# A four-direction scan whose directions run in an order that alternates with the image, with its input reloaded in blocks of 1024

## The chip, the core and the metric

The kernel runs on one core of one Trainium2 chip. The metric is the device time of one execution in microseconds (us); lower is better.

## What is computed

The input x is (8, 64, 64, 96): eight images of 64 x 64 pixels with 96 channels. Two layers are added to it, a selective scan block and a small resampling network. The change touches the scan alone, which in the reference is

```python
x_flat = xa.reshape(B, D_INNER, L)                       # B = 8, D_INNER = 192, L = 4096
x_wh = xa.transpose(0, 1, 3, 2).reshape(B, D_INNER, L)   # the same pixels by columns
x_hwwh = jnp.stack([x_flat, x_wh], axis=1)
xs = jnp.concatenate([x_hwwh, jnp.flip(x_hwwh, -1)], axis=1)   # four directions, K = 4
x_dbl = jnp.einsum('bkdl,kcd->bkcl', xs, x_proj_w)
delta = jax.nn.softplus(dts + dt_proj_b[None, :, :, None])
# each direction k, channel d, state n, along l:
h = dA * h + (dl * ul)[..., None] * Bl[:, :, None, :]
y = jnp.einsum('bkdn,bkn->bkd', h, Cl)
y = (y1 + y2 + y3 + y4)    # the four directions, turned back to row order
```

with 192 channels, 16 states, and `xs * Dk` added to each direction's y. Direction 0 goes along the rows forward, 1 along the columns forward, 2 along the rows backward, 3 along the columns backward.

## The kernel before

The program has three phases, one after the other. The first normalises x, makes `xa` (a convolution) and a gate, and leaves both in DRAM. The second, `scan_phase`, is the scan. The third adds the directions' results, projects, and computes the second layer.

**Steps and units.** The scan phase works through 256 steps in the order of the list `steps`: image b (8), direction k (4), chunk ci (4 chunks of 1024 positions), half (2 halves of 96 channels). A step is 12 units, one for each group g of 4 states and each third j of the 96 channels, 128 partitions x 1024 positions each. One image is 32 steps, one direction 8. The four directions of an image are called first to fourth here by their place in time; before the change they are k = 0, 1, 2, 3.

**A unit.** TensorE (PE) fills a PSUM tile with B spread over partitions (`fill`, the line with `selb`, L614, or with `diag`, L655 in six units of a pair of steps). VectorE (DVE) multiplies it by `dur` (L739), then scans it (L761). ScalarE (ACT) makes the decays `E` from `dlr` (L845). GpSimd (POOL) multiplies the scanned states by C (L945) and, in four units of a pair of steps, makes the product with `dur` itself into `dbu` (L937). PE sums the products of a group into `yps` (L677, in `sum_y`). Each engine works through a fixed order.

**sum_y.** For the first group of a step it begins with what is to be added to the scan's result: in direction k = 0 the skip term, a product of `dg` and `u` (L668, one call for each 512 columns); in directions k = 2 and 3, for which `second(m)` is true, the result of direction k - 2, which was stored in DRAM (`yk`) and is loaded back as `yp` (L671, also one call for each 512 columns). It stands ahead of the `fill` of a later unit on PE: at unit 5 of a step the order is fill(6), first half of `sum_y`, then fill(7), second half.

**u.** The tile `u` holds the whole of one image's `xa`, 96 partitions x 2 halves x 4096, and is not doubled. `project` (L599) reads it for B, C and dt of a chunk, POOL's `delta` (L928) for `dlu` = delta x u, and the skip term reads it. `load_u(b)` loads it with two DMAs of 1536 KB once all readers of the image before are through (`x_done`, `dlu_made`), and counts them on one semaphore, `u_in`.

**The DMA queue.** All DMAs of the scan are issued by SyncE (SP) in program order, and SP stands still where one has to wait: `out_dl` and `out_dlu` write delta and dlu of a step to DRAM, `in_dlr` and `in_dur` read them back spread over 128 partitions (4 DMAs of 384 KB each), `store_y` and `load_y` carry the results, each for the step that the loop of `sync` names. `load_u` of the next image stands in the next to last step of an image, between `out_dlu` and `in_dur` of the last step.

Of the kernel before, what the change touches and what calls it, by code (L numbers as in the profile page):

```python
# [13 lines left out]
NB = 8  # L14
HW = 64
L = HW * HW
C = 96
ND = 192
NS = 16
NK = 4  # L20
# [3 lines left out]
TC = 1024  # L24
# [284 lines left out]
def scan_phase(nc, ctx, T, S):  # L309
# [47 lines left out]

    steps = [(b, k, ci, half) for b in range(NB) for k in range(NK) for ci in range(NCH) for half in range(2)]
    NSTEP = len(steps)
# [5 lines left out]
    ve_set = sem("ve_set")  # L365
    u_in = sem("u_in")
    x_done = sem("x_done")
# [87 lines left out]
    def second(m):  # L455
        return steps[m][1] >= 2

# [3 lines left out]

    def ends_image(m):
        return m % (NK * 2 * NCH) == NK * 2 * NCH - 1

# [26 lines left out]
    def sync(e):  # L491
        for t, n in consts:
            e.dma_start(t, S[n]).then_inc(consts_in, 16)

        def load_u(b):
            if b:
                e.wait_ge(x_done, 16 * b)
                e.wait_ge(dlu_made, 32 * b)
            for h in range(2):
                e.dma_start(u[:, h, :], S["xa"][b, h]).then_inc(u_in, 16)  # L500

# [36 lines left out]
        def load_y(m):  # L538
            if m == NSTEP or not second(m):
                return  # L540
            b, k, ci, half = steps[m]
            t0 = t_of(k, ci)
            e.wait_ge(y_stored, 16 * (steps.index((b, k - 2, NCH - 1 - ci, half)) + 1))
            if seconds(m):
                e.wait_ge(yp_added, seconds(m))
            e.dma_start(yp[:], S["yk"][b, k % 2, half, :, t0:t0 + TC]).then_inc(yp_in, 16)

        load_u(0)
        for m in range(2):
# [4 lines left out]
        for n in range(NSTEP):  # L554
            if n % 2 == 0:
                if n:
                    in_dlr(n + 1)
                if n:
                    out_dlu(n + 1)
                if ends_image(n + 1) and n + 2 < NSTEP:  # L560
                    load_u(n // 32 + 1)
                if n:
                    in_dur(n + 1)
                if n:
                    store_y(n - 1)
                load_y(n + 1)
            else:
                if n + 1 < NSTEP:
# [15 lines left out]
    def tensor(e):  # L584
        def project(c, sub):
            b, k, ci, _ = steps[2 * c]
            t0 = t_of(k, ci) + sub * 512
            if sub == 0:
                if ("x", c) in held:
                    e.wait_ge(*held["x", c])  # L590
                e.wait_ge(u_in, 32 * (b + 1))
            o = stage[0:C + NR, sub * 512:(sub + 1) * 512]
# [66 lines left out]
        def sum_y(i, sub):  # L659
            m, g = divmod(i, NG)  # L660
            b, k, ci, half = steps[m]
            cols = slice(sub * 512, (sub + 1) * 512)
            if sub == 0 and g == 0 and m:
                e.wait_ge(y_copied, m)
            if g == 0 and k == 0:
                t0 = t_of(k, ci) + sub * 512
                e.wait_ge(skip_made, 3)
                e.matmul(yps[0:C, cols], dg[:, half, :], u[:, half, t0:t0 + 512], start=True, stop=False)  # L668
            if g == 0 and second(m):
                e.wait_ge(yp_in, 16 * (seconds(m) + 1))  # L670
                r = e.matmul(yps[0:C, cols], idn[0:C, 0:C], yp[:, cols], start=True, stop=False)  # L671
                if sub:
                    r.then_inc(yp_added)
            if sub == 0:
                e.wait_ge(hc_done, 3 * (i + 1))
            for j in range(NJ):
                r = e.matmul(yps[32 * j:32 * j + 32, cols], sely[:], HC[:, (3 * i + j) % NHC, cols],  # L677
                             start=g == 0 and k == 1, stop=g == NG - 1)
            if sub:
                r.then_inc(y_summed)  # L680
# [239 lines left out]
    def pool(e):  # L920
        def delta(m):
            b, k, ci, half = steps[m]
            e.wait_ge(dl_made, m + 1)
            if m:
                e.wait_ge(dlu_out, 16 * m)
                e.wait_ge(lt_done, m)
            e.wait_ge(u_in, 32 * (b + 1))
            e.tensor_tensor(shaped(dlu[:], k), shaped(dl, k), view(k, half, t_of(k, ci), TC), ALU.mult).then_inc(dlu_made)  # L928
# [827 lines left out]
```

## Time and profile before

| | us |
|---|---|
| median of 3 runs | 12264.63 (12264.1 to 12265.26) |
| the profiled execution, its own time | 12264.13 |
| its span in the profile | 12262.3 |
| first scan of the first image to the end of the last scan | 668.3 to 10353.9 |

The profile comes from one execution. Its span is 1.8 us shorter than the time of the same execution. The scan phase takes 9.7 of the 12.3 ms; in it DVE is the busiest engine.

### The profile page before, as it was taken

How to read it: one execution, taken by the hardware profiler on the slowest of the kernel's cores; microseconds unless marked ns; L12 is line 12 of the kernel's file. 1: busy time of each engine (PE TensorE's matmuls, PEld its weight loads, DVE VectorE, ACT ScalarE, POOL GpSimd, SP SyncE). 2: the span in 40 equal slices, each digit the busy share in tenths (PEclk: the TensorE clock that was granted, in tenths of full speed). 3: DMA queues.
4: the chain of work that ended last, by engine and by line, in shares of the span. 5: the costliest groups of instructions: out<-in, count | busy, mean ns of one | idle time of the engine just before them, and what ended most of it. 6: DMA issues, size and time to landing. Idle time of an engine off the chain costs nothing. (4 is left out here: it accounts for less than half of the span.)

```text
span 12262.3 us, 232157 instructions
## 1 busy us (share of the span) xinstructions
PE 10426.1 (85%) x89848; PEld 5489.9 (45%) x89848; DVE 10738.2 (88%) x6806; ACT 8077.2 (66%) x13314; POOL 9755.1 (80%) x4238
## 2 busy tenths in 40 slices
PE   8978888888888888888888888888888886899999
PEld 5633333333333333333333333333333332678778
DVE  7779999999999999999999999999999997555554
ACT  3367777777777777777777777777777775444443
POOL 2179999999999999999999999999999998433330
PEclk9977888788878887888788878887888787899999
DMA  3354554455555555555555455545555554221220
GB/s 106 106 120 114 124 135 114 115 126 135 117 117 127 134 117 117 127 133 118 119 127 133 114 117 124 132 114 118 126 131 117 122 127 115 65 60 45 63 63 12
DMA packets 380175, 1363.43 MB, mean 111 GB/s; under 512 B 55270, under 2 KB 55974, under 8 KB 375756
## 3 DMA queue, kind: packets, MB, share of 16 engines
q1 hardware_dynamic: 379084, 1348.57, 46.5%
q8 instruction: 723, 11.85, 0.4%
q14 instruction: 368, 3.01, 0.1%
HBM read 983.45 MB, written 364.90 MB: 110 GB/s over the span
## 5 line engine op out<-in xcount | busy, mean ns | idle before, releaser
L945 POOL TENSOR_TENSOR HC<-H,crep 128x1024 f32<-128x1024 f32 x3072 | 7199.2, 2370 | 525.3 <-DVE H L761 405.9
L761 DVE TENSOR_TENSOR_SCAN H<-E,car,psum 128x1024 f32<-128x1024 f32 x1920 | 4478.5, 2343 | 206.1 <-PE psum L655 120.1
L614 PE MATMUL psum<-sx,selb 96*128 96x512 f32 x4864 | 2148.0, 540 | 1360.3 <-DVE H L761 1207.6
L845 ACT ACTIVATE E<-dlr,am 128x1024 f32<-128x1024 f32 x2560 | 2907.6, 1144 | 37.1 <-DVE H L761 33.8
L677 PE MATMUL psum<-HC,sely 128*32 128x512 f32 x12288 | 2684.8, 737 | 35.8 <-POOL HC L945 35.8
L614 PEld LDWEIGHTS psum<-sx,selb 96*128 96x128 f32 x4864 | 945.7, 236 | 3225.4 <-DVE H L761 1924.5
L739 DVE TENSOR_TENSOR psum<-dur,psum 128x1024 f32<-128x1024 f32 x1792 | 2169.6, 1211 | 170.2 <-PE psum L614 167.4
L655 PE MATMUL psum<-diag,dluT 128*32 128x128 f32 x49152 | 1844.8, 307 | 200.2 <-DVE H L761 165.3
L655 PEld LDWEIGHTS psum<-diag,dluT 128*32 128x32 f32 x49152 | 1563.3, 124 | 854.7 <-DVE H L761 704.4
L761 DVE TENSOR_TENSOR_SCAN H<-E,psum 128x1024 f32<-128x1024 f32 x640 | 1455.8, 2284 | 67.1 <-PE psum L655 39.3
L829 ACT ACTIVATE diag<-idn,blt 128x128 f32<-128x128 f32 x4096 | 1292.3, 391 | 58.4 <-PE psum L655 58.0
L937 POOL TENSOR_TENSOR dbu<-dur,brep 128x1024 f32<-128x1024 f32 x512 | 1213.8, 2373 | 114.3 <-DVE H L761 68.1
L845 ACT ACTIVATE psum<-dlr,am 128x1024 f32<-128x1024 f32 x512 | 573.0, 1119 | 715.7 <-DVE H L761 712.0
L808 ACT COPY crep<-psum 128x1024 f32<-128x1024 f32 x512 | 517.0, 1010 | 606.3 <-PE psum L614 566.7
L761 DVE TENSOR_TENSOR_SCAN H<-psum,car,dbu 128x1024 f32<-128x1024 f32 x384 | 892.9, 2325 | 0.0
L851 ACT COPY car<-H 128x1 f32<-128x1 f32 x2304 | 415.3, 180 | 699.6 <-DVE H L761 699.3
L677 PEld LDWEIGHTS psum<-HC,sely 128*32 128x32 f32 x12288 | 382.7, 120 | 963.3 <-issue 748.1
L928 POOL TENSOR_TENSOR dlu<-dlt,u 96x1024 f32<-96x1024 f32 x256 | 673.7, 2632 | 161.5 <-ACT dlt L795 161.5
L608 PE MATMUL psum<-dlt,dtw 6*96 6x512 f32 x1024 | 725.9, 844 | 6.5 <-DVE sx L733 3.4
L1601 POOL TENSOR_TENSOR y<-y,tmp 96x1024 f32<-96x1024 f32 x64 | 195.2, 3109 | 454.9 <-DMA tmp<-scr_yk 454.9
L599 PE MATMUL psum<-u,wx 96*102 96x512 f32 x1024 | 463.0, 595 | 30.6 <-DMA u<-scr_xa 30.6
L1327 PEld LDWEIGHTS psum<-w2s,hs 128*100 128x100 f32 x4800 | 447.4, 168 | 15.1
(135 smaller groups left out, 10695.0 us busy)
## 6 DMA issues: line engine op xcount, KB each, us to landing
dur<-scr_dlu SPq DMA_DIRECT2D x1024, 384.0 KB, 6.8
dlr<-scr_dl SPq DMA_DIRECT2D x1024, 384.0 KB, 6.6
scr_dl<-dlt SPq DMA_DIRECT2D x256, 384.0 KB, 3.0
scr_dlu<-dlu SPq DMA_DIRECT2D x256, 384.0 KB, 8.5
scr_yk<-yt SPq DMA_DIRECT2D x256, 384.0 KB, 6.4
yp<-scr_yk SPq DMA_DIRECT2D x128, 384.0 KB, 8.8
scr_xa<-xs SPq DMA_DIRECT2D x64, 384.0 KB, 3.5
scr_sz<-xs SPq DMA_DIRECT2D x64, 384.0 KB, 3.4
```

What stands on the lines that cost most here:

```text
L608: r = e.matmul(stage[0:C, sub * 512:(sub + 1) * 512], dtw[C:C + NR, k * ND + half * C:k * ND + (half + 1) * C], dts[:, sub * 512:(sub + 1) ...
L614: r = e.matmul(o[:, sub * 512:(sub + 1) * 512], selb[:, which, :], sx[:, c % 2, sub * 512:(sub + 1) * 512], start=True, stop=True)
L655: r = e.matmul(P[un % 2][32 * q:32 * q + 32, i * 128:(i + 1) * 128], dluT[:, m % 2, i, 32 * j:32 * j + 32], diag[:, i, q, :], start=True, ...
L677: r = e.matmul(yps[32 * j:32 * j + 32, cols], sely[:], HC[:, (3 * i + j) % NHC, cols], start=g == 0 and k == 1, stop=g == NG - 1)
L739: e.tensor_tensor(P[un % 2], dur[:, slot(m, j), :], P[un % 2], ALU.mult).then_inc(mul_done)
L761: e.tensor_tensor_scan(H[:, un % NH, ::step], decay[:, ::step], drive[:, ::step], init, ALU.mult, ALU.add).then_inc(scan_done)
L808: e.copy(crep[:, REPS[i], :], stage).then_inc(rep_out)
L829: e.mul(diag[:, i // 4, i % 4, :], idn[:], blt[:, i:i + 1]).then_inc(diag_made)
L845: e.activation(o, dlr[:, slot(m, j), :], ACT.Exp, scale=am[:, ae:ae + 1]).then_inc(exp_done)
L928: e.tensor_tensor(shaped(dlu[:], k), shaped(dl, k), view(k, half, t_of(k, ci), TC), ALU.mult).then_inc(dlu_made)
L937: e.tensor_tensor(dbu[:, p % NDB, :], dur[:, slot(m, j), :], brep[:], ALU.mult).then_inc(pool_mul_done)
L945: e.tensor_tensor(HC[:, un % NHC, :], H[:, un % NH, :], crep[:, g, :], ALU.mult).then_inc(hc_done)
```

## The change

`KORDER` gives the order of the directions: 0, 1, 3, 2 in even images and 2, 1, 3, 0 in odd ones. So the fourth direction of an image and the first of the next are the same, a direction along the rows, and both go through the blocks of 1024 positions in the same order. The reload of `u` is split by `load_rows` into one DMA of 768 KB for each block (both halves of the channels), each with its own semaphore, issued as soon as the step that used the block last in the fourth direction has its y copied. `rows_wait` makes `project` and `delta` wait for the block alone, and only in an image's first direction.

```diff
+    KORDER = ((0, 1, 3, 2), (2, 1, 3, 0))
+    steps = [(b, k, ci, half) for b in range(NB) for k in KORDER[b % 2] for ci in range(NCH) for half in range(2)]
...
+    u_in = [sem(f"u_in{i}") for i in range(NCH)]
...
     def second(m):
-        return steps[m][1] >= 2
+        return m % (NK * 2 * NCH) >= 4 * NCH
...
+    def rows_wait(e, m):
+        b, k, ci, _ = steps[m]
+        if k == KORDER[b % 2][0]:
+            e.wait_ge(u_in[t_of(k, ci) // TC], 16 * (b + 1))
...
-        def load_u(b):
-            if b:
-                e.wait_ge(x_done, 16 * b)
-                e.wait_ge(dlu_made, 32 * b)
-            for h in range(2):
-                e.dma_start(u[:, h, :], S["xa"][b, h]).then_inc(u_in, 16)
+        def load_rows(b, ci):
+            t0 = t_of(KORDER[b % 2][0], ci)
+            e.dma_start(u[:, :, t0:t0 + TC], S["xa"][b, :, :, t0:t0 + TC].rearrange("h c t -> c h t")).then_inc(u_in[t0 // TC], 16)
...
-            e.wait_ge(y_stored, 16 * (steps.index((b, k - 2, NCH - 1 - ci, half)) + 1))
+            e.wait_ge(y_stored, 16 * (steps.index((b, (k + 2) % NK, NCH - 1 - ci, half)) + 1))
...
-        load_u(0)
+        for ci in range(NCH):
+            load_rows(0, ci)
...
-                if ends_image(n + 1) and n + 2 < NSTEP:
-                    load_u(n // 32 + 1)
                 if n:
                     in_dur(n + 1)
                 if n:
                     store_y(n - 1)
                 load_y(n + 1)
+                if n and steps[n - 1][1] == KORDER[steps[n - 1][0] % 2][-1] and steps[n - 1][0] + 1 < NB:
+                    e.wait_ge(y_copied, n)
+                    load_rows(steps[n - 1][0] + 1, steps[n - 1][2])
```

In `sum_y` the skip term moves behind the product with `yp`, since in odd images direction 0 is now the fourth and has both; it starts the sum only where there is no `yp`. The third direction (k = 3) now adds what the second (k = 1) has just stored; before, one other direction lay between a result and its use.

The first place is SP's queue at the end of the first image, from the `out_dl` of its last step on. Before, `u` is the tile of `load_u`:

```order
L506 DMA scr_dl<-dlt 96x1024
L516 DMA dlr<-scr_dl 32x3x1024 x4
L512 DMA scr_dlu<-dlu 96x1024
L500 DMA u<-scr_xa 96x4096 x2
L516 DMA dur<-scr_dlu 32x3x1024 x4
L536 DMA scr_yk<-yt 96x1024
L546 DMA yp<-scr_yk 96x1024
L506 DMA scr_dl<-dlt 96x1024
```

The same place in the changed kernel:

```order
L506 DMA scr_dl<-dlt 96x1024
L516 DMA dlr<-scr_dl 32x3x1024 x4
L512 DMA scr_dlu<-dlu 96x1024
L516 DMA dur<-scr_dlu 32x3x1024 x4
L536 DMA scr_yk<-yt 96x1024
L546 DMA yp<-scr_yk 96x1024
L500 DMA u<-scr_xa 96x2x1024
L506 DMA scr_dl<-dlt 96x1024
```

The load of `u` has left its place ahead of `dur` and stands, a quarter as large, behind `yp`; three more like it stand two and four steps before and two steps after this one.

The second place is PE in the first step of the fourth direction of the second image, around fill(6) and fill(7). Before, it is direction 3:

```order
L655 MATMUL psum<-diag,dluT 32x128 x32
L614 MATMUL psum<-sx,selb 128x512 x2
L655 MATMUL psum<-diag,dluT 32x128 x32
L671 MATMUL psum<-yp,idn 96x512
L677 MATMUL psum<-HC,sely 32x512 x3
L614 MATMUL psum<-sx,selb 128x512 x2
L671 MATMUL psum<-yp,idn 96x512
L677 MATMUL psum<-HC,sely 32x512 x3
```

In the changed kernel it is direction 0, and the lines are two further down, L614 being L616, L655 L657, L671 L669, L668 L675 and L677 L679:

```order
L657 MATMUL psum<-diag,dluT 32x128 x32
L616 MATMUL psum<-sx,selb 128x512 x2
L657 MATMUL psum<-diag,dluT 32x128 x32
L669 MATMUL psum<-yp,idn 96x512
L675 MATMUL psum<-u,dg 96x512
L679 MATMUL psum<-HC,sely 32x512 x3
L616 MATMUL psum<-sx,selb 128x512 x2
L669 MATMUL psum<-yp,idn 96x512
L675 MATMUL psum<-u,dg 96x512
L679 MATMUL psum<-HC,sely 32x512 x3
```

One more product, of `u` and `dg`, stands ahead of fill(7), the second L616, and one behind it. In the first direction of odd images these two are gone, since that is now direction 2.

## Rows read from the trace of the kernel before

**Rows 1.** The page: span and busy time by engine.
```profile
span 12262.3 us, 232157 instructions
PE 10426.1 (85%) x89848; PEld 5489.9 (45%) x89848; DVE 10738.2 (88%) x6806; ACT 8077.2 (66%) x13314; POOL 9755.1 (80%) x4238
```

**Rows 2.** Busy time by stretch, images one to seven: all first directions (stretch, then engines).
```profile
sum 2113.90, PE 1771.65 PEld 799.90 DVE 2028.95 ACT 1540.69 POOL 1964.16; mean PE 253.09 PEld 114.27 DVE 289.85 ACT 220.10 POOL 280.59
```

**Rows 3.** The same of the second directions: the first image, then the sum.
```profile
972.20:1272.90 300.70, 247.63 (x2235) 115.15 (x2232) 289.33 (x157) 219.49 (x369) 283.19 (x121) 0.79 0.50 117
...
sum 2109.80, PE 1742.69 PEld 812.01 DVE 2026.01 ACT 1537.16 POOL 1982.75; mean PE 248.96 PEld 116.00 DVE 289.43 ACT 219.59 POOL 283.25
```

**Rows 4.** The same of the third directions: the second image, then the sum.
```profile
2483.30:2784.40 301.10, 250.12 (x2267) 112.14 (x2264) 289.68 (x156) 220.13 (x369) 281.08 (x121) 0.85 0.53 125
...
sum 2107.90, PE 1777.36 PEld 800.83 DVE 2028.18 ACT 1538.54 POOL 1969.37; mean PE 253.91 PEld 114.40 DVE 289.74 ACT 219.79 POOL 281.34
```

**Rows 5.** The same of the fourth directions: first and last of seven, and the sum.
```profile
1572.10:1880.00 307.90, 256.37 (x2267) 116.45 (x2264) 289.79 (x156) 219.59 (x369) 284.10 (x121) 0.82 0.56 133
...
8843.40:9153.70 310.30, 258.65 (x2267) 115.08 (x2264) 289.87 (x156) 219.92 (x369) 283.71 (x121) 0.82 0.57 132
sum 2153.80, PE 1796.62 PEld 809.60 DVE 2028.31 ACT 1538.47 POOL 1986.87; mean PE 256.66 PEld 115.66 DVE 289.76 ACT 219.78 POOL 283.84
```

**Rows 6.** Timeline of SP at the end of the first image (start, us, instruction).
```profile
1796.59 0.84 SPq L500 DMA_DIRECT2D u<-scr_xa  x2
1804.88 1.73 SPq L516 DMA_DIRECT2D dur<-scr_dlu  x4
```

**Rows 7.** Timeline of POOL there, in brackets the idle time before.
```profile
1827.20 4.67 POOL L937 TENSOR_TENSOR dbu<-dur,brep 128x1024 f32<-128x1024 f32 x2 [6.09 <-DMA dur<-scr_dlu]
```

**Rows 8.** POOL's waits, 700 to 10354 us: in total, times, longest.
```profile
POOL dbu L937 <- DMA dur<-scr_dlu: 42.1, 7, 8.0
```

**Rows 9.** Timeline of SP in a step two earlier, from its y store on.
```profile
1737.10 0.32 SPq L536 DMA_DIRECT2D scr_yk<-yt  x1
1744.24 0.31 SPq L546 DMA_DIRECT2D yp<-scr_yk  x1
1765.17 0.30 SPq L506 DMA_DIRECT2D scr_dl<-dlt  x1
```

**Rows 10.** Engines in a stretch of that step; last: clock, DMA share, GB/s.
```profile
1752.00:1770.00 18.00, 16.12 (x181) 7.86 (x178) 17.87 (x11) 12.68 (x18) 18.00 (x8) 1.00 0.10 30
```

**Rows 11.** Timeline of all engines at the start of the scan phase.
```profile
610.00 0.90 SPq L500 DMA_DIRECT2D u<-scr_xa  x2
612.90 0.69 DVE L765 CAST selb<-crep 96x1024 fp32r<-96x1024 f32 x1 [28.82 <-DMA idn<-in_idn]
628.08 6.42 PE L599 MATMUL psum<-u,wx 96*102 96x512 f32 x8 [30.57 <-DMA u<-scr_xa]
```

**Rows 12.** Busy time by stretch there.
```profile
610.00:620.00 10.00, 0.00 (x0) 0.00 (x0) 1.20 (x4) 0.57 (x2) 0.00 (x0) 0.50 1.02 237
620.00:630.00 10.00, 1.92 (x3) 0.84 (x4) 0.00 (x0) 0.00 (x0) 0.00 (x0) 0.50 0.48 111
```

**Rows 13.** DMA issues: KB each, median us from issue to landing.
```profile
scr_dl<-dlt SPq DMA_DIRECT2D x256, 384.0 KB, 3.0
...
scr_yk<-yt SPq DMA_DIRECT2D x256, 384.0 KB, 6.4
yp<-scr_yk SPq DMA_DIRECT2D x128, 384.0 KB, 8.8
```

**Rows 14.** Timeline of PE and DVE, a step with half 0 of a third direction.
```profile
1364.70 1.10 PE L671 MATMUL psum<-yp,idn 96*96 96x512 f32 x2
...
1366.72 0.74 PE L614 MATMUL psum<-sx,selb 96*128 96x512 f32 x2
...
1367.49 1.23 DVE L739 TENSOR_TENSOR psum<-dur,psum 128x1024 f32<-128x1024 f32 x1 [0.26 <-PE psum L614]
```

**Rows 15.** The same in a second direction, which has neither product.
```profile
1064.78 0.73 PE L614 MATMUL psum<-sx,selb 96*128 96x512 f32 x2
...
1066.34 1.21 DVE L739 TENSOR_TENSOR psum<-dur,psum 128x1024 f32<-128x1024 f32 x1
```

More of the change, by code:

```diff
@@ L356, in scan_phase @@
     NCONST = 16 * len(consts)
-    steps = [(b, k, ci, half) for b in range(NB) for k in range(NK) for ci in range(NCH) for half in range(2)]
+    KORDER = ((0, 1, 3, 2), (2, 1, 3, 0))
+    steps = [(b, k, ci, half) for b in range(NB) for k in KORDER[b % 2] for ci in range(NCH) for half in range(2)]
     NSTEP = len(steps)
@@ L365, in scan_phase @@
     ve_set = sem("ve_set")
-    u_in = sem("u_in")
+    u_in = [sem(f"u_in{i}") for i in range(NCH)]
     x_done = sem("x_done")
@@ L460, in seconds @@
         return line * 4 * NCH + max(0, rest - 4 * NCH)
-    def ends_image(m):
-        return m % (NK * 2 * NCH) == NK * 2 * NCH - 1
+    def rows_wait(e, m):
+        b, k, ci, _ = steps[m]
+        if k == KORDER[b % 2][0]:
+            e.wait_ge(u_in[t_of(k, ci) // TC], 16 * (b + 1))
     def rep_index(c, i):
@@ L590, in project @@
                     e.wait_ge(*held["x", c])
-                e.wait_ge(u_in, 32 * (b + 1))
+                rows_wait(e, 2 * c)
             o = stage[0:C + NR, sub * 512:(sub + 1) * 512]
@@ L664, in sum_y @@
                 e.wait_ge(y_copied, m)
[L665 to L668, printed above, removed]
             if g == 0 and second(m):
@@ L673, in sum_y @@
                     r.then_inc(yp_added)
+            if g == 0 and k == 0:
+                t0 = t_of(k, ci) + sub * 512
+                e.wait_ge(skip_made, 3)
+                e.matmul(yps[0:C, cols], dg[:, half, :], u[:, half, t0:t0 + 512], start=not second(m), stop=False)
             if sub == 0:
@@ L677, in sum_y @@
                 r = e.matmul(yps[32 * j:32 * j + 32, cols], sely[:], HC[:, (3 * i + j) % NHC, cols],
-                             start=g == 0 and k == 1, stop=g == NG - 1)
+                             start=g == 0 and k != 0 and not second(m), stop=g == NG - 1)
             if sub:
@@ L926, in delta @@
                 e.wait_ge(lt_done, m)
-            e.wait_ge(u_in, 32 * (b + 1))
+            rows_wait(e, m)
             e.tensor_tensor(shaped(dlu[:], k), shaped(dl, k), view(k, half, t_of(k, ci), TC), ALU.mult).then_inc(dlu_made)
```

## The prediction

> **What bounds the kernel now.** I read the page first: over the span DVE is the busiest engine, at 88% [rows 1]. The span holds two phases that the change doesn't touch, so the next view is busy time by stretch, with a stretch for each direction of each image. In all first directions of seven images DVE is busy 2029 of 2114 us, in the second 2026 of 2110, in the third 2028 of 2108 [rows 2 to 4]: 96%, and the same work each time. The scan therefore runs at DVE's pace, and what the change is worth is what it does to the 12 us or so per direction in which DVE stands idle. In the fourth directions DVE does the same 2028 us of work, but in 2153.8 us [rows 5]. Against the mean of the other three, 2110.5, these seven directions lose 43.3 us, 6.2 each. The eighth image, which loads nothing behind it, isn't in these sums.
>
> The timeline says where. In the next to last step SP issues the 3.1 MB of u, and 8 us later the dur of the last step [rows 6]. POOL, which needs that dur, can go on only at 1827.2, 22 us after dur's issue, and has then been idle for 6.1 us [rows 7]. In the waits of POOL this is the only wait on a DMA in the scan after its start: seven times, 42.1 us together [rows 8]. Two ways of counting thus agree on 42 to 43 us. The project of the next image is not what waits, since u has landed by then; the harm is that u lies ahead of dur in one queue.
>
> The other place is the start. PE's first product of the scan waits 30.6 us, and it ends with the landing of u at 628.0. The constants, issued ahead of u, had all landed by 612.9, when DVE's first instruction could start [rows 11]. Nothing else is running, and all that follows hangs on this product.
>
> **What goes away at the ends of images.** The block loads stand behind yp, out of dur's way. In a normal step of the fourth direction yp is issued at 1744.2 and the next DMA at 1765.2 [rows 9], and from 1752 to 1770 the DMA engines are 10% busy, at 30 GB/s [rows 10]. A block is 0.79 MB; at the 237 GB/s of the start [rows 12] it takes 3.3 us, at half of that 6.6. It fits in this hole behind yp. Nothing waits for it: the block of chunk 0 is used by project only some four steps later, and each of the others likewise. Its wait for y_copied is the one that the y store ahead of it has already passed. The cost of the blocks is zero while that hole is there; without it each would delay the dl of the next step by 3 to 7 us. I take the whole 43.3 us as gained. The bounds are 0 and 45.
>
> **The start.** Only the first block must land. It begins when the constants are in, at 612.9 at the latest, and 0.79 MB at 237 GB/s is 3.3 us. A DMA of 384 KB alone takes 3.0 us to land [rows 13], which at that rate is 1.4 us more than its bytes, so the block lands at 612.9 + 3.3 + 1.4 = 617.6 instead of 628.0: 10.4 us gained. At best the 1.4 us are already in the 612.9, and it is 11.8; at worst the four blocks share the engines and the first lands with the last, and it is 0. The other three blocks are in by about 628, while the first write of delta follows some 15 us behind the first product, so they delay nothing. The Trainium skill (DMA: Bandwidth & Descriptors, Queues, rings and completion order) says that on each DMA engine descriptors are consumed in ring order, with nothing ordered across the engines. By that the first block comes first, as I assume; the order among several loads of u is shown by no row here.
>
> **What moves on PE.** The number of products is unchanged; their places are not. In odd images the skip product leaves the first direction (now 2) and joins the product with yp in the fourth (now 0). Both stand ahead of fill(7), for which DVE waits in the steps of half 0. Without either product the fill starts at 1064.78 and ends at 1065.51, 0.83 us before DVE takes it at 1066.34, without waiting [rows 15]. With one product it ends at 1367.46, and DVE has waited 0.26 us [rows 14]. So one product costs 0.8 + 0.3 = 1.1 us of PE's time there, which is also its length in the timeline, and the first one is nearly hidden while a second one has no cover left: 1.1 us in each of 4 steps of half 0, in 4 odd images, 16 x 1.1 = 17.6 us. In the steps of half 1 and for the second half of sum_y I take nothing: there the unit that follows is preceded by a multiply of its own or is one that PE doesn't fill by selb.
>
> Against it stands the first direction of odd images, which loses its product, 16 x 0.26 = 4.2 us by the same rows. But the second directions, which have neither product, are no faster: DVE is idle there for 83.8 us against 79.7 in the third [rows 3, 4]. Their clock is lower, 0.79 against 0.85, PE being idle more. So I give little of the 4.2 back, and take +14 us for both, with bounds of 0 (the second product is made up for elsewhere, as the first seems to be) and 18. The Trainium skill (TensorE: Matmul & The Clock Gate, The HAM clock gate) says that PE's resting state is 1.2 GHz and that activity releases it to 2.4 GHz. The trace agrees in direction, with the two clock figures just named. By that rule the direction with both products would run at the higher clock for longer and the one with none at the lower, and the 4.2 us vanish whole: the sum would be 17.6 instead of 14.
>
> **The y results.** Direction 3 now loads in its first step what was stored two steps before. In a step of half 1 that store is issued right ahead, and the load must wait for its landing, 6.4 us in the median [rows 13]. But before the change SP stood for 7.1 us between the same two DMAs anyway, for the yp before to be read [rows 9], and then nothing comes until 1765.2. yp is used about a step later, and lands 8.8 us after its issue. For half 0 the landing of dlu lies between the two. I take nothing; if SP were held 6 us more, 14 us of the hole would remain.
>
> **The sum**, on the profiled execution's own time of 12264.1 (its span plus 1.8; the median of the runs is 0.5 higher): 12264.1 - 43.3 - 10.4 + 14 = 12224.4. With the 0.5 that is 12225, 0.33% faster. A measurement of this kernel can tell about 0.2%, 24.5 us, from no change, that is, 12240 and 12289.
>
> **The rivals.**
> 1. *The second product on PE is hidden.* For it: the third directions, with a product, take no longer than the second, without. Against: fill(7) is already late with one. Then 12264.1 - 43.3 - 10.4 = 12210.
> 2. *The first block doesn't land early*, because four loads issued within 2 us run side by side. For it: the trace has no such case at an idle queue. Against: the constants, issued first, were in 15 us ahead of u. Then 12225 + 10.4 = 12235.
> 3. *The ends of images don't get shorter.* The blocks take dur's or dl's place in the queue, or the 6 us have a second cause that comes up as soon as this one is gone. For it: four more transfers per image. Against: the hole of rows 10 and the equal sums. Then 12225 + 43.3 = 12268, no change.
> 4. *PE becomes the bound in the fourth directions of odd images, and the kernel is slower.* There are two skip products in each of 8 steps and 4 images, 64 in all. At the lower clock each takes twice 1.1 us; with all of it on the way, 64 x 2.2 = 141 us, and 12210 + 141 = 12351. It decides from 79 us on, 1.2 us a product. Against: PE is 83% busy in these stretches [rows 5], and only one in four of these places has DVE waiting.
>
> **How the numbers follow.** My forecast (12225, of its own range 12214 to 12235) has 0.58, rival 1 0.18, rival 2 0.09, rival 3 0.10, rival 4 0.05. The range reaches down past rival 1 by what the start may give more and by the few us by which sums of single directions scatter (the first directions differ by 6.0 us in rows 2 from the third in rows 4 with equal work), and up past rival 2: 12205 to 12240. It leaves out rivals 3 and 4. Faster by over 0.2%: forecast and rivals 1 and 2, less their tail, 0.84. Within 0.2%: rival 3 and the tail, 0.11. Slower: 0.05.
>
> **What would show it.** Right: no wait of POOL for dur after the start; the fourth directions of even images as long as the third, near 301 us; PE's first product at about 617.6; the fourth directions of odd images some 4 us longer than those of even ones, with DVE waiting 1.3 to 1.4 us for fill(7) in steps of half 0. Wrong: fourth directions that stay near 307 us in even images (rival 3), a first product near 628 (rival 2), equal fourth directions in even and odd images (rival 1), or waits for PE at every group in odd ones (rival 4). What I know least is how much of a delay on PE the next steps give back.

## The result and the profile after

The changed kernel takes 12194.1 us (median of 4 runs, 12186.3 to 12202.7) against 12264.4 for the kernel before on the same chip; the ratio is 0.9945 (0.9928 to 0.9962). It is 0.55% faster where 0.33% was forecast, and lies below the range. The profiled executions stand at 12192.6 and 12264.1 us, 71.5 apart. The span after, from the page:

```profile
span 12190.8 us, 231878 instructions
```

Busy time by stretch, fourth directions of the first and the second image and the sum of seven (stretch, length; PE, PEld, DVE, ACT, POOL; clock, DMA share, GB/s), which answers to [rows 5]:

```profile
1562.70:1863.30 300.60, 255.49 (x2267) 114.30 (x2264) 289.57 (x156) 219.62 (x369) 280.56 (x121) 0.82 0.57 133
2764.40:3063.20 298.80, 257.83 (x2304) 114.71 (x2304) 289.38 (x157) 221.02 (x369) 280.08 (x121) 0.87 0.57 133
...
sum 2109.50, PE 1795.85 PEld 802.36 DVE 2026.44 ACT 1541.60 POOL 1962.65; mean PE 256.55 PEld 114.62 DVE 289.49 ACT 220.23 POOL 280.38
```

The seven fourth directions have gone from 2153.8 to 2109.5 us with the same work of DVE: 44.3 us, where 43.3 were forecast. All waits of POOL between 700 and 10288 us, against [rows 8]:

```profile
POOL HC L947 <- DVE H L763: 371.2, 450, 1.8
POOL HC L947 <- ACT crep L810: 119.2, 127, 1.9
POOL dbu L939 <- DVE H L763: 71.4, 86, 4.2
POOL dlu L930 <- ACT dlt L797: 28.3, 98, 0.3
POOL HC L947 <- issue: 0.3, 1, 0.3
```

No wait for a DMA is among them. The timeline of SP shows a block's load where it was expected, behind yp and 20 us ahead of the next DMA, as against [rows 9]:

```profile
1727.13 0.32 SPq L536 DMA_DIRECT2D scr_yk<-yt  x1
1734.29 0.31 SPq L546 DMA_DIRECT2D yp<-scr_yk  x1
1734.65 0.43 SPq L500 DMA_DIRECT2D u<-scr_xa  x1
1755.22 0.30 SPq L506 DMA_DIRECT2D scr_dl<-dlt  x1
```

At the start, to be read against [rows 11]:

```profile
607.99 2.47 SPq L500 DMA_DIRECT2D u<-scr_xa  x4
611.94 0.28 ACT L863 ACTIVATE am<-am 128x96 f32<-128x96 f32 x1 [6.18 <-DMA idn<-in_idn]
...
615.99 2.00 PE L601 MATMUL psum<-u,wx 96*102 96x512 f32 x2 [20.45 <-DMA u<-scr_xa]
```

The constants were in by 611.9. The first product starts 8.0 us after u's first DMA is issued, before it was 18.1: 10.1 us gained of the 10.4 forecast. The trace has the landings of the four blocks too, at 615.9, 619.3, 622.6 and 625.0 us, in the order of their issue.

So the 71.5 us are: 44.3 in the fourth directions of seven images and 10.1 at the start, both as forecast; 8.8 in all other directions, 2.0 in the phase ahead of the scan, 0.7 between first product and first scan, and 5.6 in the phase behind it, which the forecast doesn't have; and nothing at all of the 14 us that PE was to cost. Between the 12224.4 forecast and the 12192.6 measured lie 31.8 us: these 14, and 17.8 of which all but 1 us stand in places that no term held.

The cost on PE is there where it was looked for, and still doesn't count. Timeline of PE and of DVE in the fourth direction of the second image, at the place of [rows 14]:

```profile
2855.59 1.10 PE L669 MATMUL psum<-yp,idn 96*96 96x512 f32 x2
2856.53 1.02 PE L675 MATMUL psum<-u,dg 96*96 96x512 f32 x2
2857.48 1.06 PE L679 MATMUL psum<-HC,sely 128*32 128x512 f32 x6
2858.47 0.74 PE L616 MATMUL psum<-sx,selb 96*128 96x512 f32 x2
...
2859.25 1.23 DVE L741 TENSOR_TENSOR psum<-dur,psum 128x1024 f32<-128x1024 f32 x1 [1.17 <-PE psum L616]
```

DVE waits 1.17 us for fill(7), 0.9 more than with one product. Yet this direction is the shorter one of the two above, 298.8 against 300.6 us, and its mean granted clock is 0.87 against 0.82.

### The profile page after: what moved, and what is told of

Read it like the earlier page. It is cut to its first block and busy times, and to the rows that moved or that the text cites. A ratio compares the mean times of both kernels' runs of the same rounds, so it can differ in the third digit from the quotient of the medians.

```text
span 12190.8 us, 231878 instructions
## 1 busy us (share of the span) xinstructions
PE 10416.3 (85%) x89848; PEld 5493.1 (45%) x89848; DVE 10733.1 (88%) x6806; ACT 8079.8 (66%) x13314; POOL 9756.1 (80%) x4238
## 5 line engine op out<-in xcount | busy, mean ns | idle before, releaser
L616 PE MATMUL psum<-sx,selb 96*128 96x512 f32 x4864 | 2153.7, 541 | 1363.9 <-DVE H L763 1202.1
L679 PE MATMUL psum<-HC,sely 128*32 128x512 f32 x12288 | 2693.0, 739 | 8.2 <-POOL HC L947 8.0
L616 PEld LDWEIGHTS psum<-sx,selb 96*128 96x128 f32 x4864 | 946.5, 236 | 3225.5 <-DVE H L763 1964.0
L657 PE MATMUL psum<-diag,dluT 128*32 128x128 f32 x49152 | 1836.7, 306 | 177.1 <-DVE H L763 159.8
L657 PEld LDWEIGHTS psum<-diag,dluT 128*32 128x32 f32 x49152 | 1563.4, 124 | 834.1 <-DVE H L763 713.7
L679 PEld LDWEIGHTS psum<-HC,sely 128*32 128x32 f32 x12288 | 383.9, 120 | 901.7 <-issue 713.2
L610 PE MATMUL psum<-dlt,dtw 6*96 6x512 f32 x1024 | 714.8, 832 | 6.7 <-DVE sx L735 3.4
```

Of the source, the lines that this page charges most:

```text
L610: r = e.matmul(stage[0:C, sub * 512:(sub + 1) * 512], dtw[C:C + NR, k * ND + half * C:k * ND + (half + 1) * C], dts[:, sub * 512:(sub + 1) ...
L616: r = e.matmul(o[:, sub * 512:(sub + 1) * 512], selb[:, which, :], sx[:, c % 2, sub * 512:(sub + 1) * 512], start=True, stop=True)
L657: r = e.matmul(P[un % 2][32 * q:32 * q + 32, i * 128:(i + 1) * 128], dluT[:, m % 2, i, 32 * j:32 * j + 32], diag[:, i, q, :], start=True, ...
```

## The experiments

All ratios are to the kernel before on the same chip, with their 95% interval. Theory 1 is the forecast without its PE term: what was gained is dur's place in the queue and the first block, and the rest is scatter; its rival is that the changed order of the directions gains something itself. Theories C and F came up on the way and are told in the expectations. "Scan" is the time from the first to the end of the last scan of the profiled execution, 9685.6 us before and 9632.5 after.

**The two kernels again.** No edit.

> The kernel before, unchanged, for a second profile. Theory 1, that what the 43 and 10 us didn't explain (the first and third phases 8 us, the second and third directions 10 us) is scatter between executions: the sums of directions over seven images differ from the first profile's by up to 10 us with no change in the program, the fourth directions stay near 2154 us, and the total lies within 0.1% of 12264. Rival, that the changed order really shortens the second and third directions: here their sums stay at 2110 and 2108 within 2 us.

> The changed kernel, unchanged, for a second profile and a closer ratio. Theory 1 (scatter): the total lies between 12186 and 12212, with direction sums that move by up to 10 us against its first profile. Rival: second and third directions at 2104 us again, and the total at 12193 within 3 us. Both: first product of the scan some 11.5 us after the first constant's DMA is issued, and no wait of GpSimd for dur after the start.

The kernel before came to 12258 us, ratio 1.0002 (0.9993 to 1.0011), its scan to 9679.2; its own runs on that chip reached from 12242.7 to 12280.0. POOL waits for dur seven times, 42.5 us, and the seven fourth directions sum to 2142.3. The changed kernel came to 12199.6 us, ratio 0.9952 (0.9939 to 0.9964), its scan to 9626.1, with fourth directions of 2101.5. The sums of directions move by 3 to 12 us between executions of one program, more than was expected for the fourth, and the time up to u's first DMA and the third phase by 2 and 3 us. The rival falls: in the kernel before the second and third directions sum to 2112.8 and 2103.2 instead of 2110 and 2108, and in the changed one they are at 2108.7 and 2107.6 instead of 2104.

**The order alone.** u is loaded whole at its old place (`load_u` and its one semaphore are back, which the lines below leave out), the skip product stays in the first direction.

```diff
+                if (n + 1) % 32 == 31 and n + 2 < NSTEP:
+                    load_u(n // 32 + 1)
                 if n:
                     in_dur(n + 1)
...
-                if n and steps[n - 1][1] == KORDER[steps[n - 1][0] % 2][-1] and steps[n - 1][0] + 1 < NB:
-                    e.wait_ge(y_copied, n)
-                    load_rows(steps[n - 1][0] + 1, steps[n - 1][2])
...
-            if g == 0 and k == 0:
+            if g == 0 and k == KORDER[b % 2][0]:
```

> The alternating order of the directions alone: u is loaded whole, where the kernel before loads it, and the skip product stays in an image's first direction, since u is overwritten before the fourth ends. Theory 1 (only the queue and the start matter, the order itself is worth nothing): 12264 within 10 us, fourth directions near 2154 us over seven images, GpSimd waits for dur seven times, 42 us. Rival, that the order itself gives the 10 us more that were measured: about 12252, with second and third directions of 2104 us.

12270 us, ratio 1.0007 (0.9998 to 1.0015); seven waits for dur, 45.2 us; fourth directions 2158.4, and second and third ones of 2111.5 and 2115.6, where the rival had 2104. The order by itself gives nothing; it only makes the block loads possible.

**u behind dur in the kernel before.**

```diff
-                if ends_image(n + 1) and n + 2 < NSTEP:
-                    load_u(n // 32 + 1)
                 if n:
                     in_dur(n + 1)
+                if ends_image(n + 1) and n + 2 < NSTEP:
+                    load_u(n // 32 + 1)
```

> The kernel before with one statement moved: the whole load of u stands behind the dur of the image's last step instead of ahead of it. Theory 1 (the 6 us per image are dur's place behind u in the queue): 12264 - 43 = 12221, fourth directions near 2110 us over seven images, no wait for dur; u then lands about when its first reader needs it, which may give back up to 2 us per image, 14 us. Rival, that 3.1 MB at the end of an image cost the same wherever they stand in the queue, and blocks are what is needed: 12264, with the wait moved to project or to yp.

12228 us, ratio 0.9979 (0.9970 to 0.9988). The waits for dur are gone, and the fourth directions come to 2124.1 us. That is 29.7 us less than in the first profile of the kernel before, where the blocks gave 44.3, and 23.9 less than the mean of its two, where they gave 42.5: somewhat over half of the way. PE now waits for u, five times:

```profile
PE psum L599 <- DMA u<-scr_xa: 10.5, 5, 2.4
```

So the place in the queue was the cause. From behind dur the 3.1 MB are late for the next project instead; no other place for them was tried. The blocks bring the rest.

**The first reader waits for all four blocks.**

```diff
-            e.wait_ge(u_in[t_of(k, ci) // TC], 16 * (b + 1))
+            for i in range(NCH) if b == 0 and ci == 0 else (t_of(k, ci) // TC,):
+                e.wait_ge(u_in[i], 16 * (b + 1))
```

> The changed kernel, but the first reader of u in the first image waits for all four blocks. Both theories of the start agree that the first block's early landing is what was gained: the first product starts 20 to 21 us after the first constant's DMA instead of 11.2, 10 us more in all. If the blocks ran side by side, the first landing with the last, it would stay at 11.2.

The first product starts at 624.4 us, 19.7 after the first constant's DMA, against 11.5 and 11.0 in the two profiles of the changed kernel: 8.5 us of the expected 10. The blocks land one behind the other, here at 615.0, 618.5, 621.8 and 624.3 us. In the total, 12201.4 us with runs from 12189.7 to 12221.8, this can't be seen.

**The skip product out of the fourth directions.**

```diff
-            if g == 0 and k == 0:
+            if g == 0 and k == KORDER[b % 2][0]:
...
-                e.matmul(yps[0:C, cols], dg[:, half, :], u[:, half, t0:t0 + 512], start=not second(m), stop=False)
+                e.matmul(yps[0:C, cols], dg[:, half, :], u[:, half, t0:t0 + 512], start=True, stop=False)
...
-                             start=g == 0 and k != 0 and not second(m), stop=g == NG - 1)
+                             start=g == 0 and k == 1, stop=g == NG - 1)
```

> The changed kernel with the skip product kept in the first direction of every image (direction 2 in odd ones), so that no step has two products ahead of fill(7); the result is the same sum. My term of the prediction: the second product costs 14 us, so this would be 14 us faster than the changed kernel, with fourth directions of odd images at 300.3 us and DVE's wait for fill(7) at 0.3 us there. Theory C (the second product's 1.1 us are paid back by a higher granted clock in the rest of the step pair): the same time as the changed kernel within 5 us, fourth directions of odd images 1 to 2 us longer than with the second product (300.3 against 298.7), clock there 0.82 instead of 0.87.

12217.6 us, ratio 0.9968 (0.9955 to 0.9980), 18 us slower than the changed kernel where my term had it 14 faster and theory C equal. The fourth directions of odd images are at 300.5, 300.3 and 300.6 us, as theory C had it; the loss is in the first directions of odd images, 303.7 to 303.9 against 300.2. Neither theory explains that, and the trace shows what happens there. Timeline of skip_first in such a direction, PE and DVE:

```profile
2104.54 1.94 PE L657 MATMUL psum<-diag,dluT 128*32 128x128 f32 x60
2108.01 0.41 PE L657 MATMUL psum<-diag,dluT 128*32 128x128 f32 x4 [1.54 <-issue]
...
2108.48 2.35 DVE L763 TENSOR_TENSOR_SCAN H<-E,car,psum 128x1024 f32<-128x1024 f32 x1 [2.08 <-PE psum L657]
...
2112.37 1.23 DVE L741 TENSOR_TENSOR psum<-dur,psum 128x1024 f32<-128x1024 f32 x1 [1.55 <-PE psum L616]
```

PE stands still in the middle of a diag fill, 4 matmuls before its end, and waits for nothing that the profile shows; the granted clock falls behind it (0.66 from 2109 to 2114 us), and DVE loses 3.6 us in two waits. The DMA rows of the page show queues of kind "instruction", here of the changed kernel:

```profile
q8 instruction: 722, 11.83, 0.4%
q14 instruction: 366, 3.00, 0.1%
```

That is 16 KB a packet on q8. The packets themselves, read from the trace for all such stalls of over 0.6 us inside a diag fill:

```
kernel         stalls   PE goes on after the end of a q8 packet (min, median, max us)   the same for 500 random diag matmuls, median
before           20     1.21  1.40  1.71                                                8.2
changed          10     1.21  1.40  1.59                                                8.8
skip_first       25     1.20  1.37  1.53                                                8.1
after_pad128     23     1.28  1.42  1.58                                                8.8
```

Each time PE goes on 1.2 to 1.7 us after a piece of instructions has landed; of the random matmuls some 11 to 14% stand within 1.8 us of one. So PE has run out of instructions. In all diag fills of the scan these stalls come to

```profile
PE psum L655 <- issue: 32.1, 22, 4.4
```

in the kernel before, and

```profile
PE psum L657 <- issue: 14.6, 11, 2.7
```

in the changed one, in 14.6 us instead of 32.1. This is theory F: which diag fill meets the end of a piece just when the data DMAs are dense is a matter of where the pieces end in the stream of instructions, which any edit on PE shifts. That dense data DMAs are what makes a piece late is a supposition; no run isolates it.

**Work on PE at other places.** warm_behind puts a useless product of 32 columns behind fill(7) in the directions that have none, third_ahead the same product ahead of fill(7) in the fourth directions of odd images (the condition is then `g == 0 and sub == 0 and k == 0 and second(m)`). Here is the edit of warm_behind:

```diff
+            if g == 0 and sub == 1 and k != 0 and not second(m):
+                t0 = t_of(k, ci) + sub * 512
+                e.wait_ge(skip_made, 3)
+                e.matmul(yps[C:128, cols], dg[:, half, 0:32], u[:, half, t0:t0 + 512], start=True, stop=True)
```

> The changed kernel with a useless product of 32 columns of dg with u, into rows of PSUM that nobody reads, in the directions that have neither skip nor yp product, in the second half of sum_y alone, where it stands behind fill(7). Theory C (clock): the granted clock rises there from 0.78 to 0.80 or more, the delta products of half 1 get shorter, and these 12 directions take 299 to 300 us instead of 300.3, 5 to 15 us in all. Rival (slack: work on PE ahead of a fill is absorbed by a wait that is there anyway, whatever the clock): no direction gets shorter, and the time is that of the changed kernel or up to 10 us more.

> The changed kernel with a third product of the same length, useless, ahead of fill(7) in the fourth directions of odd images, which already have two and the highest clock, 0.87. Theory C (clock): the clock has little left to give, so the 1.1 us show: DVE waits 2.4 us for fill(7) in 16 steps, these directions take 302 to 303 us instead of 298.7, 12 to 17 us in all. Rival (slack): they stay at 299 us and the time at that of the changed kernel.

12209.7 us (0.9963, 0.9949 to 0.9976) and 12197.0 us (0.9953, 0.9940 to 0.9965). Neither tells the theories apart, since the product takes no time of its own. In warm_behind the clock didn't rise either: its mean over the 12 directions is 0.78, and they take 3609.8 us together, within the 3604.8 to 3619.9 of the six profiles that have the changed kernel's scan (after, after_again, the three shifted ones below and wait_all_start). In third_ahead the fourth directions of odd images take 298.6, 302.8 and 299.8 us. Timeline of PE there (L679 is the useless product, L683 those with sely, which start 0.96 us behind L675, against 0.95 without it):

```profile
2854.31 1.02 PE L675 MATMUL psum<-u,dg 96*96 96x512 f32 x2
2855.26 0.62 PE L679 MATMUL psum<-u,dg 96*32 96x512 f32 x1
2855.27 0.63 PE L683 MATMUL psum<-HC,sely 128*32 128x512 f32 x3
```

With all its 96 columns it does take time (in the first 512 positions of these steps the skip then counts twice):

```diff
-                e.matmul(yps[0:C, cols], dg[:, half, :], u[:, half, t0:t0 + 512], start=not second(m), stop=False)
+                for _ in range(2 if second(m) and sub == 0 else 1):
+                    e.matmul(yps[0:C, cols], dg[:, half, :], u[:, half, t0:t0 + 512], start=not second(m), stop=False)
```

> The third product again, as third_ahead showed none of its length: its 32 columns ran beside the products with sely. Here the skip product with all its 96 columns is repeated ahead of fill(7) in the fourth directions of odd images (so the skip counts one and a half times there). Theory C (the second product is paid back by the clock, which then has little left): DVE waits 2.1 us for fill(7) in 16 steps, and these directions take 301 to 303 us, 10 to 16 us in all. Rival (slack): 299 us as with two products.

12219.4 us, ratio 0.9970 (0.9958 to 0.9982). DVE waits 2.1 us for fill(7) in the middle of these steps, and the fourth directions of odd images take 306.6, 303.4 and 304.1 us, at a clock of 0.87 to 0.88: 4.2 us more than the mean of 300.5 for two products. That looks like 4 steps of 1 us, but isn't all the product's. In each of these three directions PE also has one of the stalls of theory F, of 2.0, 1.8 and 1.4 us. Directions with two products and a stall of 1.4 us or more take 302.2 to 303.1 us, 302.7 in the mean of seven (the same six profiles), which leaves 2.0 us for the third product. The eighth image, not in these sums, has no stall in third_wide and takes 299.1 us in its fourth direction; with two products and no stall it takes 297.5 to 298.2 in three profiles, 1.3 us less in the mean. So the third product delays fill(7) by 0.9 us in four steps and costs 1 to 2 us a direction, not 4.2. The run stands at one place of the stream only.

**The stream of PE shifted.** Fulfilled waits on PE ahead of its first product, 64, 128 or 192 of them:

```diff
         e.wait_ge(consts_in, NCONST)
+        for _ in range(128):
+            e.wait_ge(consts_in, NCONST)
         e.wait_ge(ve_set, 1)
```

> The changed kernel with 64 already fulfilled waits on PE ahead of its first product, which fill a time in which PE waits for u anyway and shift all that follows in PE's stream of instructions by 64 against the 16 KB pieces in which the trace shows it being fetched. Theory F (in the scan PE stands in the middle of its diag fills for its next instructions, and how often depends on where the pieces end against the bursts of data DMAs): those stalls, 14.6 and 16.6 us in two profiles of the changed kernel and 32.1 and 29.6 us in two of the one before, take another value between 10 and 35 us, and the scan's length follows it by about 1 us for 1. Rival (the stalls are fewer because u no longer loads in one piece, wherever the pieces end): they stay between 13 and 18 us, and the time within 5 us of the changed kernel's.

> The same with 128 such waits, half a piece, which delay the first product by some 3 us. Theory F: stalls of another value between 10 and 35 us, and a scan longer by the difference. Rival: 13 to 18 us, and the time of the changed kernel plus the 3 us.

> The kernel before with 128 such waits, which fit into its longer wait for u. Theory F: the stalls leave the 29.6 to 32.1 us of its two profiles by 5 us or more, most likely downwards, and the total by as much. Rival: 29 to 33 us, and 12260.

> The kernel before with 64 fulfilled waits on PE ahead of its first product. Theory F (the stalls of PE for instructions follow the place in the stream): stalls between 15 and 35 us, scan between 9662 and 9686 us, lower where the stalls are. Rival (the stalls belong to the kernel): 30 to 32 us, 9680.

> The same with 192. Theory F as for 64. With it the kernel before stands at four places; I expect the mean of its scans at 9676 us, 5 below that of the two first profiles.

> The changed kernel with 192 such waits, which delay its first product by about 4 us. Theory F: stalls between 15 and 35 us, scan between 9627 and 9650. With it the mean over four places should be 9635 us, 41 below that of the kernel before: what the ends of images give (43.3), with nothing lost or gained on PE.

> The variant with the skip product in every image's first direction, its stream shifted by 64 waits. Theory F: the 15 us by which its scan was longer than the changed kernel's (9644.7 against 9626 to 9632), with 31 us of stalls, were mostly the stream's place: stalls below 27 and a scan of 9628 to 9640. Rival (the product ahead of fill(7) in the first directions costs 3.5 us in each odd image): 9645 again, with first directions of odd images at 303.7.

What came out, with the sums of PE's stalls without a visible cause in the scan (all lines), and of the seven fourth directions (where two profiles exist, their mean):

```
                      total us   ratio (interval)             stalls us   scan us   fourth directions
before, 0             12260      -                            34.3        9682.4    2148.0
before, 64 waits      12254.5    0.9998 (0.9989 to 1.0007)    29.1        9664.4    2140.1
before, 128           12246.4    0.9992 (0.9983 to 1.0001)    23.5        9669.1    2146.4
before, 192           12254.7    0.9994 (0.9985 to 1.0003)    32.0        9678.7    2148.0
changed, 0            12199.6    0.9952 (0.9939 to 0.9964)    18.3        9629.3    2105.5
changed, 64           12197.7    0.9952 (0.9940 to 0.9965)    28.2        9629.3    2107.9
changed, 128          12209.2    0.9964 (0.9951 to 0.9976)    35.6        9648.5    2105.5
changed, 192          12215.9    0.9961 (0.9949 to 0.9974)    34.1        9639.9    2099.5
skip_first, 0         12217.6    0.9968 (0.9955 to 0.9980)    31.1        9644.7    2109.6
skip_first, 64        12198.7    0.9950 (0.9937 to 0.9962)    23.5        9624.0    2102.8
```

The waits themselves delay the changed kernel's first product by 2 us at 128 and by 5.5 at 192. What the rival said of the stalls is refuted (its time, within 5 us of the changed kernel's, did hold at 64 waits): over their profiles the stalls are 23.5 to 36 us in the kernel before and 17 to 36 in the changed one, by place alone, and their means over four places are equal, 29.7 and 29.0 us. The mean scans are 9673.6 and 9636.8 us, 37 apart (with 43 for the ends of images and nothing on PE, 43 would be the forecast). The fourth directions are apart by 41.0 us in the mean (2145.6 and 2104.6), and by 32 to 49 at the single places; the rest of the scan, which in the first pair of profiles had given 8.8 us, is 4 us longer in the mean. And skip_first, moved by 64 waits, is as fast as the changed kernel, its scan 4 us shorter than expected, and the first directions of odd images at 299.4, 302.3 and 301.0 us: its 18 us were most likely the place, not the product, though the two intervals (0.9955 to 0.9980, 0.9937 to 0.9962) just overlap. "1 us for 1" didn't hold: with 28.2 us of stalls the changed kernel's scan is no longer than with 18.3. That a stall counts only where DVE has no fill in hand is my reading of it. The intervals of the totals also overlap within each kernel, so a single place's effect on the time is seen in the stalls and the scans more than in the runs.

## Why the prediction was wrong, point by point

- **The bound and the 43.3 us at the ends of images** were right: 44.3 us in the first pair of profiles, 41.0 as a mean over four places, POOL's wait for dur gone. dur_first and order_only show that the place of u in the queue is the cause; with the blocks all of it goes, with u behind dur somewhat over half.
- **The start** was right: 10.1 us against 10.4. The blocks land in the order of their issue, 2.4 to 3.4 us apart, and wait_all_start shows by its 8.5 us that the early landing of the first is the gain. This agrees with the rule of the Trainium skill that I named (DMA: Bandwidth & Descriptors, Queues, rings and completion order), by which each DMA engine consumes descriptors in ring order.
- **The 14 us of PE's second product** are the step that failed. The delay at fill(7) was sized nearly right: 0.9 us of the 1.1, and DVE's wait there 1.17 us against the 1.3 to 1.4 forecast. What was wrong is that it was taken for a cost of the direction, 16 x 1.1 us less a little, with nothing to pay it back. The fourth directions of odd images are as long as those of even ones: 300.5 us (18 directions) and 300.9 (24), over the changed kernel at its four places, its second profile and wait_all_start. Where PE has no stall in them (0.3 us or less in all), those with two products are even the shorter ones: 298.9 us (9 directions) against 300.3 (13). I had read off a local wait and multiplied it, though the third directions, with one product, were already no longer than the second, without. Rival 1 (12210, with 0.18) was the right case.
- **Why it is paid back.** With one product DVE waits not only at fill(7) in the steps of half 0, but also at fill(10) in the steps of half 1. That wait stood in the trace of the kernel before, in a fourth direction:

```profile
1789.53 1.23 DVE L739 TENSOR_TENSOR psum<-dur,psum 128x1024 f32<-128x1024 f32 x1 [0.97 <-PE psum L614]
```

  The prediction took nothing in half 1. Ahead of fill(10) PE has fill(9), six products with sely and four delta products (L610). Here is this place in the fourth direction of the second image, first skip_first, which has one product there:

```profile
2896.95 2.35 DVE L763 TENSOR_TENSOR_SCAN H<-E,car,psum 128x1024 f32<-128x1024 f32 x1
...
2902.86 1.22 PE L616 MATMUL psum<-sx,selb 96*128 96x512 f32 x2 [2.11 <-DVE H L763]
2904.01 1.93 PE L679 MATMUL psum<-HC,sely 128*32 128x512 f32 x6
2905.87 3.72 PE L610 MATMUL psum<-dlt,dtw 6*96 6x512 f32 x4
2909.52 1.22 PE L616 MATMUL psum<-sx,selb 96*128 96x512 f32 x2
...
2910.78 1.23 DVE L741 TENSOR_TENSOR psum<-dur,psum 128x1024 f32<-128x1024 f32 x1 [0.97 <-PE psum L616]
```

  then the changed kernel, which has two:

```profile
2892.61 2.35 DVE L763 TENSOR_TENSOR_SCAN H<-E,car,psum 128x1024 f32<-128x1024 f32 x1
...
2898.52 0.74 PE L616 MATMUL psum<-sx,selb 96*128 96x512 f32 x2 [1.41 <-DVE H L763]
2899.18 1.06 PE L679 MATMUL psum<-HC,sely 128*32 128x512 f32 x6
2900.17 3.61 PE L610 MATMUL psum<-dlt,dtw 6*96 6x512 f32 x4
2903.71 1.22 PE L616 MATMUL psum<-sx,selb 96*128 96x512 f32 x2
...
2905.39 1.21 DVE L741 TENSOR_TENSOR psum<-dur,psum 128x1024 f32<-128x1024 f32 x1
```

  Both times fill(9) starts 5.91 us after the same scan of DVE, the first line. From there to the first delta product PE takes 3.01 us with one product and 1.65 with two, and in the second case DVE doesn't wait. The granted clock of these stretches is 0.50, the lower of the two levels (1.2 GHz), and 1.00, the upper one (2.4 GHz); before them PE had been idle for 2.11 and 1.41 us. In the 18 profiles of all kernels the clock between these two points is at 0.55 or less in 1775 places, and DVE waits 0.96 to 1.09 us for fill(10) in every one; it is at 0.95 or more in 383, and DVE waits in none. With two products it is at the upper level in all 72 places of the six profiles, with one in 10 of 96, and in the fourth directions of odd images of skip_first and skip_first_pad64, with one, in 5 of 24. So theory C is shown for this wait: PE starts no earlier, it works at the upper clock, and up to 4 waits of 1 us a direction go, against four delays of 0.9 us. Slack alone, with PE at the same clock, would leave fill(10) as late as it was. DVE's waits for PE in the whole direction, skip_first first:

```profile
DVE psum L741 <- PE psum L616: 4.2, 7, 1.1
DVE H L763 <- PE psum L657: 3.8, 6, 1.1
...
DVE psum L741 <- PE psum L616: 5.0, 5, 1.2
DVE H L763 <- PE psum L657: 1.8, 5, 0.8
```

  Those for the diag fills (L657) fall by 2 us as well, and the direction is 298.8 instead of 300.5 us long. How much of these 2 us is the clock's, and which of PE's work holds it up, the runs don't isolate: in the second directions, with neither product, PE had been idle for only 1.0 us at this place, and the clock was low in all 192. The third product finds no wait at fill(10) left to remove, and costs 1 to 2 us. The rule of the Trainium skill on the clock (TensorE: Matmul & The Clock Gate, The HAM clock gate), that activity releases it, agrees with the 72 of 72 against 10 of 96; I had used it only to take 4 us of credit away.
- **What no term held**: the place of PE's instructions, and scatter. By the means over four places the change is worth 37 us in the scan and 10 at the start, some 47 us or 0.38%; the ratios of the runs, averaged over the places of each kernel, give 0.39%. The sum without its PE term was 53.7; with it, 39.7. In the build that was timed the kernel before stood 9 us worse than its mean and the changed one 8 us better, some 16 us of the 70. That is an estimate and not shown as the place's alone: all places but the first have one profile, two profiles of one build differ by 6.4 us in the scan, and of the kernel before no shifted build is clear of no change in its runs. The remaining 7.6 us in the first and third phases of the first pair are scatter: the third phase was 1902.8 to 1917.0 us long over 18 profiles of both kernels and their variants, in no order. So the kernel got faster for the reasons forecast; how far below the range the time fell is the failed term together with the luck of this build.
- **The range** was too narrow on the low side for that reason. It allowed a few us for scatter, where executions of one program spread by up to 46 us (after_pad192, 12192.8 to 12238.6) and the scans of the four places by 18 to 19.

## What to carry over

When a whole tile is reloaded at once, look at what stands behind it in the same queue; the reader of the tile may be in time while another transfer isn't. An order of work in which the last user of a block is followed by its first, and the load cut to those blocks, takes the load out of the way. A delay read at one wait isn't a cost until a whole period is longer by it: compare periods with and without the work first, and only such as have the same stalls in them. Look also at the waits further on: work that keeps PE at the upper clock can remove one of them. And below half a per cent, compare a kernel at several places of its instruction stream before an effect is given to an edit on PE.

## What was not expected of the hardware

- PE runs out of instructions in the scan 11 to 32 times, mostly inside fills of 64 short matmuls, for up to 4.4 us, and goes on 1.2 to 1.7 us after a 16 KB packet of q8 has landed. The stalls add up to 13 to 36 us, and 64 instructions more moved them by 10.
- A product into output rows 96 to 127 ran beside products into rows 0 to 95 that stood behind it: 0.62 us and 0.63 us from 2855.26 and 2855.27 on, with no delay of what followed. The same product with 96 columns delayed fill(7) by 0.9 us.
- One more product in each half of `sum_y` had the granted clock at 1.00 instead of 0.50 some 4 us behind it, in the same step: fill(9) and the six products behind it took 1.65 us instead of 3.01, and the direction with more work on PE was the shorter one, 298.9 us against 300.3 without stalls.
